# A third PSUM bank for attention scores, with k turned in the bank of out, a shorter norm chain on VectorE and all low parts on GpSimd

## The reference

```
xn = layernorm(x)
q, k, v = xn @ Wq.T, xn @ Wk.T, xn @ Wv.T
q = q * rsqrt(mean(q*q) + 1e-6) * q_norm_w;  k likewise with k_norm_w      # per head
scores = q k^T / sqrt(128) + slope[head] * (key - query), masked above the diagonal
s = softmax(scores) v, heads joined, @ Wo.T
g = silu(2 * sum_h softmax_h(...) * low-rank map h of xn)
y = x + s * g
```

## Time and profile before

| | |
|---|---|
| median of three runs | 804.32 us (803.34 to 804.47) |
| profiled execution | 802.56 us, its span 800.6 us, 2.0 us around it |
| PE busy | 751.1 us (94%) |
| DVE, ACT, POOL busy | 580.5, 571.5, 360.5 us (73, 71, 45%) |
| chain that ended last | PE 75%, DVE 9%, issue 7%, ACT 6% |
| granted TensorE clock | 1.00 through the loop, 0.52 at 756.8 to 758.5 us |

### The profile page before, as it was taken

One profiled execution on the slowest core, in us unless ns is written; L12 is line 12 of the kernel. 1 busy time (PEld: TensorE's weight loads), 2 busy tenths in 40 slices (PEclk: granted clock), 3 DMA queues, 4 the chain that ended last, 5 costly groups with the idle time before them and its releaser, 6 DMA issues.

```text
span 800.6 us, 14772 instructions
## 1 busy us (share of the span) xinstructions
PE 751.1 (94%) x4029; PEld 636.2 (79%) x4029; DVE 580.5 (73%) x1461; ACT 571.5 (71%) x1370; POOL 360.5 (45%) x278
## 2 busy tenths in 40 slices
PE   7888999999999999989999999999999899999897
PEld 6776878878787888878788787878888787888775
DVE  7857767777785777777687777858777786876755
ACT  3657777677776877677776777768776777767863
POOL 4323463364444355244632644444552446426274
PEclk9999999999999999999999999999999999999999
DMA  7015747266454636437462664646464374626521
GB/s 281 2 31 128 211 99 205 67 154 175 118 157 112 175 107 180 122 93 210 112 189 67 152 175 119 157 112 176 106 180 121 94 210 112 189 66 155 175 80 66
DMA packets 148467, 108.93 MB, mean 136 GB/s; under 512 B 44096, under 2 KB 139200, under 8 KB 148288
## 3 DMA queue, kind: packets, MB, share of 16 engines
q1 hardware_dynamic: 148416, 108.43, 50.6%
HBM read 66.18 MB, written 42.21 MB: 135 GB/s over the span
## 4 chain that ended last, share of the span: by engine, by line
PE 75%; DVE 9%; issue 7%; ACT 6%; DMA 1%; DVEq 0%; POOL 0%; SPq 0%; ACTq 0%
PE qkv_ps L1068 10%; PE qkv_ps L1069 9%; PE qkv_ps L1070 9%; PE out_ps L1068 7%; PE out_ps L1070 7%; PE out_ps L1069 7%; PE turn_ps L1177 4%; PE score_ps L1068 4%; PE score_ps L1070 3%; PE score_ps L1069 3%; PE mix_ps L1068 3%; PE mix_ps L1069 3%; PE mix_ps L1070 3%; DVE qk_norm L887 3%; PE score_ps L1164 2%
## 5 line engine op out<-in xcount | busy, mean ns | idle before, releaser
L460 POOL TENSOR_TENSOR pt_lo<-x_sb,pt_hi 128x512 fp32r<-128x512 f32 x123 | 163.6, 1353 | 235.8 <-ACT pt_hi L616 235.8
L827 DVE CUSTOM_DVE_ANT_0 probs<-score_ps,cst,slope 128x128 f32<-128x128 f32 (+3 forms) x256 | 131.8, 548 | 155.4 <-PE score_ps L1070 127.2
L573 ACT ACTIVATE probs<-probs,neg_max 128x128 f32<-128x128 f32 (+3 forms) x256 | 141.7, 554 | 78.3 <-DVE neg_max L827 78.2
L1068 PE MATMUL qkv_ps<-w_hi,xt_hi 128*128 128x512 f32 (+1 forms) x512 | 180.0, 351 | 3.9 <-DVE w_lo L769 1.5
L1069 PE MATMUL qkv_ps<-w_lo,xt_hi 128*128 128x512 f32 (+1 forms) x512 | 173.5, 339 | 0.0
L1070 PE MATMUL qkv_ps<-w_hi,xt_lo 128*128 128x512 f32 (+1 forms) x512 | 172.7, 337 | 0.0
L581 ACT ACTIVATE probs<-probs,recip 128x128 f32<-128x128 f32 (+3 forms) x252 | 127.6, 553 | 54.9 <-DVE recip L834 54.9
L452 POOL TENSOR_TENSOR inv_rms<-mean_sq,minus_half 128x5 f32<-128x5 f32 x64 | 75.0, 1172 | 114.8 <-DVE mean_sq L873 113.2
L1068 PEld LDWEIGHTS qkv_ps<-w_hi,xt_hi 128*128 128x128 f32 x512 | 97.1, 190 | 17.6 <-DVE w_lo L769 1.7
L1069 PEld LDWEIGHTS qkv_ps<-w_lo,xt_hi 128*128 128x128 f32 x512 | 97.2, 190 | 10.9
L1070 PEld LDWEIGHTS qkv_ps<-w_hi,xt_lo 128*128 128x128 f32 x512 | 96.5, 188 | 11.6
(11 more groups left out here) (135 smaller groups left out, 1489.4 us busy)
## 6 DMA issues: line engine op xcount, KB each, us to landing
turning<-squared SPq DMA_DIRECT2D x120, 128.0 KB, 2.4
x_sb<-turning SPq DMA_DIRECT2D x30, 512.0 KB, 4.7
w_raw<-wqkv SPq DMA_DIRECT2D x32, 384.0 KB, 4.7
turning<-squared SPq DMA_DIRECT2D x120, 96.0 KB, 2.0
x_sb<-turning SPq DMA_DIRECT2D x30, 384.0 KB, 3.6
turning<-squared SPq DMA_DIRECT2D x128, 64.0 KB, 1.8
x_sb<-turning SPq DMA_DIRECT2D x32, 256.0 KB, 3.0
wo_raw<-wo SPq DMA_DIRECT2D x14, 512.0 KB, 5.5
```

The costliest lines, as they stand in the source:

```text
L460: nc.gpsimd.tensor_tensor(by_quad(pt_lo, j), moved_block(t, j), by_quad(pt_hi, j).bitcast(F32), ALU.subtract).then_inc(pt_lo_by_pool, 1)
L573: nc.scalar.activation(probs[:, h, 0:n], probs[:, h, 0:n], ACT.Exp, bias=neg_max[:, h:h + 1], scale=-1.0, accum_out=total[:, h:h + 1]).the ...
L827: nc.vector.tensor_tensor_reduce(probs[:, h, 0:n], score_ps[:, h % 2, 0:n], cst[:, C_DIST + SEQ - n:C_DIST + SEQ], slope[:, h:h + 1], HUGE ...
L1068: pe.matmul(out, a_hi, b_hi, start=start, stop=False)
```

## The change

Scores get a third bank (score_ps has three, turn_ps one), and the four heads come in a row on PE ahead of out. Head 3 uses the bank of head 0, so it waits for bias 0 of its own unit; head 0 waits for the last bias of the unit before. q is turned in the one bank of turn_ps; k is turned in the bank of out (out_ps), so turn_k waits until add_out of unit t-3 has read that bank.

In the norm chain, the epsilon is set once as a 129th column of the squares, the mean's factor goes into the constants, and so L873 is gone; POOL makes the power straight from the sums and also the multiplication by the factor. DVE has only the row sums and qk_norm left of the chain. The orders change: on DVE biases 2 and 3 come right after the row sums, ahead of v_lo and reciprocals 0; slope and factor are set earlier; add_out comes ahead of both square_probs; q_lo and k_lo come ahead of o_lo. On ACT exponentials 2 and 3 come right after 0 and 1, and q_hi and k_hi ahead of o_hi. POOL makes all four low parts of units with four key blocks.

```diff
-        score_ps = psum("score_ps", [2, 512])
-        turn_ps = psum("turn_ps", [2, 512])
+        score_ps = psum("score_ps", [3, 512])
+        turn_ps = psum("turn_ps", [512])
...
+        def k_turn_ps(u, left):
+
+            if u < 3:
+                return score_ps[:, 2, 0:P]
+            return qkv_ps[:, 1, 0:P] if left == 1 and u == BLOCKS - 1 else out_ps[:, 0:P]
+
+        def score_bank(t, h):
+
+            return score_ps[:, h % (3 if t >= 2 else 2), 0:keys_of(t) * P]
...
+            nc.gpsimd.memset(squares[:, :, HD:HD + 1], HD * RMS_EPS).then_inc(eps_set, 1)
...
-                pool.wait_ge(mean_sq_ready, ONE(g, u, 1))
-                nc.gpsimd.tensor_tensor(inv_rms[:, :], mean_sq[:, :], minus_half[:, 0:NORMED],
+                pool.wait_ge(sums_ready, ONE(g, u, 1))
+                nc.gpsimd.tensor_tensor(inv_rms[:, :], sums[:, :], minus_half[:, 0:NORMED],
                                         ALU.pow).then_inc(inv_rms_ready, 1)
+                pool.wait_ge(inv_rms_ready, ONE(g, u, 1))
+                pool.wait_ge(factor_set, g + (u // BLOCKS + 1))
+                nc.gpsimd.tensor_tensor(inv[:, :], inv_rms[:, :], factor[:, :], ALU.mult).then_inc(inv_ready, 1)
...
-                    if t % QB < QB - 1 or j not in LO_BY_DVE:
-                        pool.wait_ge(pt_hi_ready, PER_KEY_BLOCK(g, t, j + 1))
...
+                    pool.wait_ge(pt_hi_ready, PER_KEY_BLOCK(g, t, j + 1))
```

In the slot of ACT:

```diff
                 if here(t, left):
                     exponentials(g, t, range(0, 2))
+                if here(t, left):
+                    exponentials(g, t, range(2, HPG))
                 if w_due and t % BLOCKS == 6:
                     split_w(g + 1, range(2, 3))
                 if here(t, left):
                     normalize_probs(g, t, range(0, 2))
-                    exponentials(g, t, range(2, HPG))
...
+                if here(t + 1, left):
+                    turned_qk_hi(g, t + 1, left)
                 if here(t - 2, left):
                     mixed_hi(g, t - 2, left)
-                if here(t + 1, left):
-                    turned_qk_hi(g, t + 1)
```

In the slot of DVE:

```diff
-                    mean_square(g, t + 1)
+                    square_sums(g, t + 1)
+                if here(t, left):
+                    bias(g, t, 2)
+                    bias(g, t, 3)
+                if (t + 1) % BLOCKS == 0 and here(t + 1, left):
+                    set_slope(g, t + 1)
+                if here(t + 1, left):
                     value_lo(g, t + 1)
                 if here(t, left):
                     reciprocals(g, t, 0)
-                    bias(g, t, 2)
-                    bias(g, t, 3)
...
+                if here(t + 1, left):
+                    turned_qk_lo(g, t + 1, left)
                 if here(t - 2, left):
                     mixed_lo(g, t - 2, left)
-                if here(t + 1, left):
-                    turned_qk_lo(g, t + 1)
-                if here(t - 1, left) and (t - 1) % QB == QB - 1:
-                    moved_lo(g, t - 1)
```

On PE, the waits of the scores, turn_k and the slot:

```diff
-                if t > 0 or h >= 2:
-                    pe.wait_ge(biased_ready, PER_HEAD(g, t, h - 1))
...
+                elif h == 0:
+                    pe.wait_ge(biased_ready, PER_HEAD(g, t, 0))
+                elif h == 3:
+                    pe.wait_ge(biased_ready, PER_HEAD(g, t, 1))
+                out = score_bank(t, h)
...
-            def turn_k(g, u):
+            def turn_k(g, u, left=GROUPS):
 
-                pe.transpose(turn_ps[:, 1, 0:P], qk_norm[:, HPG, :], ident).then_inc(qk_turned, 1)
+                if left == 1 and u == BLOCKS - 1:
+                    pe.wait_ge(v_lo_ready, ONE(g, u, 1))
+                elif u > 3:
+                    pe.wait_ge(acc_ready, 1 + ONE(g, u - 4, 1))
+                pe.transpose(k_turn_ps(u, left), qk_norm[:, HPG, :], ident).then_inc(qk_turned, 1)
...
                 if here(t, left):
-                    scores(g, t, 0)
-                    scores(g, t, 1)
+                    for h in range(HPG):
+                        scores(g, t, h)
                 if here(t - 3, left):
                     out(g, t - 3)
-                if here(t, left):
-                    scores(g, t, 2)
-                    scores(g, t, 3)
```

More of the change, by code:

```diff
@@ L93, in constants @@
     c[:, C_SLOPE:C_FACTOR] = slopes
-    f = np.ones((GROUPS, NORMED))
-    f[:, :HPG] = -1.0 / (slopes.astype(np.float64).reshape(GROUPS, HPG) * math.sqrt(HD))
+    f = np.full((GROUPS, NORMED), math.sqrt(HD))
+    f[:, :HPG] = -1.0 / slopes.astype(np.float64).reshape(GROUPS, HPG)
     c[:, C_FACTOR:] = f.reshape(1, -1)
@@ L229, in build @@
         half_set = sem("half_set")
+        eps_set = sem("eps_set")
         bn_done = sem("bn_done")
@@ L587, in mixed_hi, with turned_qk_hi @@
                 nc.scalar.activation(o_part(o_hi, u, left), mixed(u, left), ACT.Copy).then_inc(o_hi_ready, 1)
-            def turned_qk_hi(g, u):
+            def turned_qk_hi(g, u, left=GROUPS):
                 b, ui = u // QB % BATCH, u % QB
-                q_ps, k_ps = turn_ps[:, 0, :], turn_ps[:, 1, 0:P]
+                q_ps, k_ps = turn_ps[:, :], k_turn_ps(u, left)
                 act.wait_ge(qk_turned, TWO(g, u, 1))
@@ L671, in end @@
                 mixed_hi(g, before - 2, 1)
-                turned_qk_hi(g, last)
+                turned_qk_hi(g, last, 1)
                 normalize_probs(g, before, range(2, HPG), late_probs)
@@ L917, in slot @@
             def slot(g, t, left):
-                if t % BLOCKS == 0 and here(t, left):
-                    set_slope(g, t)
                 if here(t, left):
@@ L929, in slot @@
                     reciprocals(g, t, 0)
-                    bias(g, t, 2)
-                    bias(g, t, 3)
                 if here(t + 1, left):
                     normalize_qk(g, t + 1)
+                if (t + 2) % BLOCKS == 0 and here(t + 2, left):
+                    set_factor(g, t + 2)
                 if here(t, left):
                     reciprocals(g, t, 2)
-                    square_probs(g, t, 0)
                 if here(t - 3, left):
@@ L951, in end @@
                 bias(g, before, 1)
-                mean_square(g, last)
+                square_sums(g, last)
                 value_lo(g, last)
@@ L960, in end @@
                 mixed_lo(g, before - 2, 1)
-                turned_qk_lo(g, last)
+                turned_qk_lo(g, last, 1)
                 add_out(g, before - 2)
@@ L995, in _ @@
             moments_of(2)
-            mean_square(0, 0)
+            square_sums(0, 0)
             normalize_x(2)
@@ L1156, in scores @@
                         pe.wait_ge(k_full_ready, PER_BATCH(g, t, 1))
-                if t > 0 or h >= 2:
-                    pe.wait_ge(biased_ready, PER_HEAD(g, t, h - 1))
-                if t < 2 and h == 0:
-                    pe.wait_ge(lt_lo_done, t + 1)
-                out = score_ps[:, h % 2, 0:n]
+                if t < 2:
+                    if t > 0 or h >= 2:
+                        pe.wait_ge(biased_ready, PER_HEAD(g, t, h - 1))
+                    if h == 0:
+                        pe.wait_ge(lt_lo_done, t + 1)
+                elif h == 0:
[3 more added lines that the diff above has]
+                out = score_bank(t, h)
                 if t % QB == 0:
@@ L1245, in slot @@
                     turn_q(g, t + 1)
-                    turn_k(g, t + 1)
+                    turn_k(g, t + 1, left)
                 if here(t + 2, left):
@@ L1259, in end @@
                 turn_q(g, last)
-                turn_k(g, last)
+                turn_k(g, last, 1)
                 out(g, before - 2)
```

59 lines of the change are left out of this document (22 added, 37 removed).

## The result

| | median | runs | profiled execution: own time, span |
|---|---|---|---|
| before | 804.39 us | 803.34 to 804.95, 4 runs | 802.56, 800.6 |
| changed | 792.06 us | 788.89 to 793.51, 4 runs | 791.87, 789.7 |

The ratio is 0.9849, 95% interval 0.9827 to 0.9871: 12.3 us faster, where 4.8 was forecast. The time is inside the range, the direction is right, and the gain is 2.6 times the forecast.

A forecast was written before the change was run, and what follows sets the result against it. PE was taken as the bound, waiting 31.4 us before turn_q. 26.3 - 14.0 - 10.8 + 3.3 = 4.8 us less gave 797.8 profiled, 799.5 us median; forecast 795 to 802.5, range 787 to 806.

The forecast's parts named there:

- Part 1: PE's gaps before turn_q in slots 2, 3, 6 and 7 go or shrink, since qk_norm comes earlier: 26.3 us gained.
- The product on POOL: Norm chain's multiplication by the factor, moved to POOL: taken as 0.35, between bounds 0.19 and 0.62.
- Part 2: PE stands before head 3 until bias 0 frees the bank: 14.0 us lost over slots of 128, 256 and 384 keys.
- The lower bound of 9: Least loss for head 3's wait for bias 0, if the release from DVE to PE is 0.06.
- Part 3: At the loop's return head 3 waits for DVE's late bias 0: 1.8 lost six times, 10.8 us.
- The bound "nothing": No loss at the loop's return, if what takes the 2.65 begins ahead of DVE's last instruction and ends by then.
- the half of rival 1: PE's gaps go and only the return of the loop stays hidden: 788.7 us, chance 0.2.
- Part 4: Waits of turn_k for add_out, and POOL's added low parts in slots 0 and 4, stay hidden: no cost.
- rival 3: POOL late in slots 1 and 5, power behind four low parts: 0.5 lost in 14 slots, 806.5 us, chance 0.03.
- Part 5: Tail: shorter gap before turn_q without a clock fall, 1.4, and inv ahead of POOL's low parts, 1.0; 3.3 us gained.
- the 1.4 for a clock that doesn't fall: Tail, behind the gap before turn_q: transposes 0.4 and first matmuls of project some 1.0 faster.
- the eighth of the slots 3: One of eight gaps before turn_q in slot 3 said to go, 0.67 + 0.2 each, 7.0 us in all.

The follow-up runs named there:

- e5: Changed kernel with head 3 of units with 128 or 256 keys placed beside head 2 in the third score bank: 778.19 us, ratio to before 0.9683.
- e1: Changed kernel with three empty instructions added to each slot of DVE's loop (24, body 302 instead of 278): 803.34 us, ratio to before 0.9995.
- e14: Kernel before with 64 empty instructions ahead of DVE's whole program, old order and loop body kept: 809.15 us, ratio to before 1.0076.
- e6: Changed kernel with w_hi's last chunk made ahead of the probabilities of heads 2 and 3 in slot 6: 785.05 us, ratio to before 0.9788.
- e13: e1 with 64 more empty instructions ahead of DVE's whole program: 796.4 us, ratio to before 0.9924.
- e11: Kernel before with only the norm chain moved to POOL, low parts and order as before: 802.6 us, ratio to before 0.9982.
- e12: Changed kernel, loop body untouched, with 8 empty instructions ahead of DVE's whole program: 813.79 us, ratio to before 1.0140.
- e10: Changed kernel with two empty instructions added to each slot of DVE's loop (body 294): 802.0 us, ratio to before 0.998.

## Why the prediction was right or wrong

- **Part 1, the norm chain and the score order: right.** Forecast for the loop were 1.41 a pass over slots 6 and 7 and 2.21 over 2 and 3, less 0.1 for head 3 in each pair: 3.42. The intervals give 1.46 (5-6 and 6-7) and 2.19 (1-2 and 2-3). The product on POOL took 0.20, the lower bound, and not 0.35. The 0.20 wait for k_lo of unit 3, said to stay, went.
- **Part 2, head 3 waits for bias 0: right in sum.** 128 keys cost 0.45 (0.6 forecast), 256 keys 0.42 (0.3). That is 12.2 us of 12.6 forecast for these two, of which the list of waits shows 3.3; e5, which takes only this wait away, gave 12.5. The lower bound of 9 doesn't follow from its own condition (0.08 less at each of 42 waits makes 10.6), which nothing rests on.
- **Part 3, the return of the loop: this step failed, and it is the largest error.** "Now head 3 waits for it", six times 1.8, 10.8 us. The chain of reasons held, and e1 shows the 1.8. But it took the 2.65 of the earlier trace rows for a property of the return. It was a property of this program's layout, and the change itself altered the layout: DVE's body lost 23 instructions and its prologue 10. The bound "nothing" stood in the text for a wrong reason, that what takes the 2.65 might begin earlier. The branch that would have hit is the half of rival 1, 788.7, in which the return costs nothing.
- **Part 4, what is hidden: right** inside the loop. Neither turn_k nor mix waits there, and rival 3, POOL late, shows nowhere.
- **Part 5, the tail: wrong sign.** The two terms came: the gap fell from 2.29 to 1.04 with no fall of the clock, and inv took 0.20. Not looked at was what comes next. PE came to out sooner, and ACT stood on a DMA with o_hi queued behind it; the wait for o_lo went from 0.50 us in the kernel before to 3.21 and the clock fell behind it. The step that failed is the 1.4 for a clock that doesn't fall, and the gap beside it, counted in full: in e14 the clock doesn't fall behind turn_q either, and PE stands the time out at out instead, so it doesn't reach the end. Forecast +3.3, measured -1.3 beside the 0.4 of the 3-4 interval.
- **The prologue: forecast 0.9 gained (the eighth of the slots 3), measured 0.9 lost.** PE comes to turn_q earlier and stands 2.17 there instead of 1.75; then the clock falls. In e1, e6 and e13, where it didn't, the same interval is 11.7 and not 13.3, so the fall costs 1.6.

By the prediction's own terms, without Part 3's: 15.6 us. The tail and the prologue missed by 4.6 and 1.7, and the seven passes were 2.0 better than their terms (7 x 0.29, from the two points on Parts 1 and 2): 11.3; less the 0.4 of the last group's 3-4 interval, which no term had, that is the 10.9 by which the spans differ. That the time lies inside the range is owed to these two misses: they took back 6.3 of the 10.8 that Part 3 had wrongly charged, and without them the time would be near 786, below the range. What the measurement leaves open is why the clock falls behind one stop of 2.17 and not behind another of 2.17; and why the fetch stops DVE for 3.1 to 3.3 us where the body ends just past the boundary (448) and for 2.4 to 2.8 where it ends 8 or more further on.

## What to carry to other kernels

Before costing a stall at a loop's return, look at the count of instruction packets on the page (here 42 where the loop was refetched in each pass, 11 or 12 where it wasn't): where a loop is refetched or near it, any edit to that engine, even one ahead of the loop, can add or remove the stall. Count the position of the loop's end in each engine's program, and try a few empty instructions in front before believing that an edit was good or bad. A stall that the old order hides is no gain to remove alone (e14, e11) and the full price in an order that waits for it (e1). And where work moves forward, follow each queue to the next thing that is then late, in the tail above all.

## What the runs showed of the hardware that was not expected

- Eight instructions that run once, ahead of the loop, cost 2.3 to 4.1 us at each of six returns: 813.8 against 792.1 us in all.
- PE's stop at the return costs twice: 2.2 us of waiting, then some 1.7 us more where the granted clock goes to 0.50 (interval 15.9, where the wait and the plain interval make 14.1; the one return of e12 at which the clock held, behind 2.08, takes 14.2).
- A clock fall isn't a function of the stop alone: it came behind 1.76 us in e1 and not behind 1.72 in e10, both ways behind 2.17, and not behind 2.55 in e14 or 3.27 in e11, both before turn_q in the tail.
- A wait of PE can stand in no list of waits: with 256 keys head 3 shows no idle and costs 0.42 us a slot.
